# Moving half of a transpose from key tile 1 to key tile 3 in two groups of a two-layer attention kernel

## What is computed

```
xn = layer_norm(x, norm_w, norm_b)
q, k, v = xn @ q_w + q_b, xn @ k_w + k_b, xn @ v_w + v_b      # 16 heads
att = softmax(q k^T + mask)                                   # no scale
y = att v
h = layer_norm(y, sb_norm_w, sb_norm_b) * (1 + scale) + shift # from the condition
x = x + silu(h) @ out_w + out_b
```

## Time and profile before

| | |
|---|---|
| median of three runs | 494.33 us |
| the profiled execution, its own time | 494.05 us |
| its span, first to last instruction | 492.2 us |
| granted TensorE clock | 1.000 |
| PE busy | 481.6 us (98%) |
| DVE busy | 387.1 us (79%) |
| ACT busy | 342.9 us (70%) |
| POOL busy | 314.1 us (64%) |

### The profile page before, as it was taken

The page is one execution under the profiler, slowest core; times in us unless marked ns, Lnnn a source line. Parts: engine busy times, 40 slices in busy tenths (PEclk is TensorE's granted clock), DMA queues, the critical chain, the costliest instruction groups (busy, mean ns, idle before and its releaser), DMA issues.

```text
span 492.2 us, 9721 instructions
## 1 busy us (share of the span) xinstructions
PE 481.6 (98%) x3205; PEld 176.6 (36%) x3205; DVE 387.1 (79%) x990; ACT 342.9 (70%) x676; POOL 314.1 (64%) x447
## 2 busy tenths in 40 slices
PE   8999899999999999999999999999999999999996
PEld 3553322323333234323343234333333323332234
DVE  3767896998887688957887588966899999999224
ACT  1662557898767685967768676776787778777853
POOL 6469976788798987898747881749971055005501
PEclk9999999999999999999999999999999999999999
DMA  7775156344413455234512451114311121111011
GB/s 254 198 200 188 50 149 246 111 124 147 128 49 113 142 149 148 69 87 121 138 39 67 134 159 43 46 46 128 89 45 44 45 88 45 44 45 45 2 43 43
DMA packets 41577, 49.79 MB, mean 101 GB/s; under 512 B 12388, under 2 KB 34036, under 8 KB 41272
## 3 DMA queue, kind: packets, MB, share of 16 engines
q1 hardware_dynamic: 33336, 31.84, 22.6%
q0 software_dynamic: 7904, 16.03, 10.7%
q10 hardware_dynamic: 288, 1.31, 0.8%
HBM read 27.62 MB, written 19.01 MB: 95 GB/s over the span
## 4 chain that ended last, share of the span: by engine, by line
PE 80%; DVE 13%; issue 3%; POOL 2%; ACT 1%; DVEq 0%; POOLq 0%; ACTq 0%
PE bank L602 20%; PE bank L648 12%; PE bank L585 12%; PE bank L576 11%; PE bank L564 9%; DVE masked L958 8%; PE bank L659 6%; PE bank L676 5%; DVE row_max L961 2%; PE bank L633 2%; PE bank L617 1%; PE bank L610 1%; ACT probs L787 1%; PE bank L734 1%; POOL shift L1335 1%
## 5 line engine op out<-in xcount | busy, mean ns | idle before, releaser
L787 ACT ACTIVATE probs<-bank 128x512 f32<-128x512 f32 x512 | 270.8, 600 | 71.6 <-PE bank L576 70.9
L961 DVE TENSOR_REDUCE row_max<-bank 128x1 f32<-128x512 f32 x256 | 160.4, 682 | 38.2 <-PE bank L585 37.9
L585 PE MATMUL bank<-k_s,q_s 64*128 64x512 f16 x512 | 180.9, 382 | 2.2 <-DVE row_max L961 1.2
L958 DVE CUSTOM_DVE_ANT_0 masked<-bank,mask_bias 128x512 bf16<-128x512 f32 x256 | 162.6, 686 | 18.9 <-PE bank L585 18.1
L564 PE MATMUL bank<-q_s,k_s 64*128 64x512 f16 x512 | 151.4, 380 | 0.3
L576 PE MATMUL bank<-shift,kx 64*128 64x512 f16 x512 | 148.7, 376 | 0.0
L602 PE MATMUL bank<-probs,v_aug 128*17 128x512 f32 x1024 | 135.5, 598 | 0.7 <-ACT probs L787 0.7
L585 PEld LDWEIGHTS bank<-k_s,q_s 64*128 64x128 f16 x512 | 46.2, 93 | 158.0 <-DVE row_max L961 66.3
L1238 POOL TENSOR_SCALAR scaled<-row_max 128x16 f32<-128x16 f32 x30 | 7.7, 255 | 87.8 <-DVE row_max L958 49.6
L648 PE MATMUL bank<-xT,wqkv 128*128 128x512 f32 x128 | 61.7, 612 | 0.9 <-DVE xT L1095 0.6
L576 PEld LDWEIGHTS bank<-shift,kx 64*128 64x128 f16 x512 | 46.9, 95 | 32.7
(11 more groups left out here) (122 smaller groups left out, 481.2 us busy)
## 6 DMA issues: line engine op xcount, KB each, us to landing
q_s<-q_parts SPq DMA_DIRECT2D x32, 256.0 KB, 3.6
k_s<-k_parts SPq DMA_DIRECT2D x32, 256.0 KB, 4.3
k_parts<-parts POOLq DMA_DIRECT2D x62, 128.0 KB, 3.2
q_parts<-parts POOLq DMA_DIRECT2D x60, 128.0 KB, 3.0
X<-in_x SPq DMA_DIRECT2D x4, 512.0 KB, 7.4
O<-oT SPq DMA_DIRECT2D x64, 32.0 KB, 2.0
roped<-inverses SPq DMA_DIRECT2D x16, 128.0 KB
y<-X SPq DMA_DIRECT2D x7, 256.0 KB, 2.2
```

Source lines behind the costliest of these rows:

```text
L585: nc.tensor.matmul(bank, m.q_s[slot][rows, i, queries], m.k_s[slot][rows, i, :], start=True, stop=True).then_inc(q.d_made, 1)
L787: act.activation(m.probs[k][:, h, :], bank, ACT.Exp, scale=1.0 if s >= B * NG else float(DH) ** -0.5)\
L958: dve.tensor_tensor_reduce(m.masked[D["max", n, k, h] % ND][:, :], bank, m.mask_bias[:, b, :], 1.0, LOWEST, ALU.add, ALU.max, to)\
L961: dve.tensor_reduce(to, bank, AX.X, ALU.max).then_inc(q.d_done, 1)
```

## The change

In groups 22 and 26 the first half of the turn stays in key tile 0. The second half goes from key tile 1 to key tile 3 of the same group. With it go its DVE operation, its tanh on ACT and its places in DVE's bank ring. The order on POOL is not edited.

```diff
-PIECES[22] = (*one(turn("f1", 0)), (), ())
+PIECES[22] = (turn("f1", 0)[:1], (), (), turn("f1", 0)[1:])
 PIECES[23] = ((), (), y(1, 0)[:1], ())
 PIECES[24] = ((), (), (), y(1, 0)[1:])
-PIECES[26] = (*one(turn("f1", 1)), (), ())
+PIECES[26] = (turn("f1", 1)[:1], (), (), turn("f1", 1)[1:])
```

## The result

Over 20 runs of each, the changed kernel takes 495.51 us (median), the kernel before 494.40: 1.11 us more, ratio 1.0025 with a 95% interval of 1.0017 to 1.0032. The forecast was 495.0, in a range of 493.8 to 495.7. A second comparison, 11 runs of the changed kernel against 27, gave 495.25 against 494.40, ratio 1.0015 (1.0006 to 1.0024). So the change costs something near the 0.2% line: the first ratio lies just over it, where I had 16%, the second under it, and both intervals hold it. In the first comparison 8 of the 20 runs of the changed kernel took over 496 us, against 2 of 20 of the kernel before; without them the medians are 495.20 and 494.40, 0.80 us apart.

A forecast was written before the change was run, and what follows sets the result against it. PE, 98% busy, was taken to bound the kernel. Per group -0.09 - 0.32 + 0.61 + 0.15 = +0.35, so +0.70 us on the profiled 494.05 gives 494.75; with 0.28 to the median, 495.0, range 493.8 to 495.7.

The forecast's parts named there:

- Key tile 1 held by ACT through L610: Group 22: the turn of the shift rows waits for ACT's late probability, so losing 0.60 us of transposes gains only 0.09.
- Key tile 2: Groups 22 and 26: without the second tanh and halving ahead, it falls from 3.42 to about 3.10 us, gaining 0.32.
- Key tile 3: Groups 22 and 26: taking in the half turn, it grows from 2.49 to 3.10 us, losing 0.61.
- Key tile 0 of group 23: Behind the turned key tile, the last score's load waits for ACT's backlog to about 2.02; 0.15 us lost (0 to 0.20).
- POOL: Negated maxima of group 24, needed in key tile 1 of group 23: slack shrinks from 1.9 to 0.3 us but holds.
- A reading that does not carry: Sign in key tile 1: a row score waits for DVE, read as DVE being behind by its second halving.
- The sum: Per group -0.09 - 0.32 + 0.61 + 0.15 = +0.35 us; group 26 the same, so +0.70.
- The gain: Rival: waits in groups 22 and 26 go, nothing replaces them; 0.38 us gained per group, 493.6 us; 12%.
- The draw: Rival: key tile 1 gives back 0.18, group 23's wait is hidden; -0.3 to +0.3 us, 494.3; 12%.
- the further waits: Rival: waits beyond the bounds, such as key tile 3's halving pushing row maxima against the three-bank ring; above +1.0 us; 5%.
- The late POOL: Rival: negated maxima of groups 24 and 28 miss L610 and PE stands; 0.5 us lost per group, 496.0 us; 9%.

The follow-up runs named there:

- the later tanhs: Kernel before, each tanh one step later on ACT: in groups 22 and 26, 493.73 against 494.17 us (repeat 494.18 against 494.40); with group 30 too, 494.87 against 494.47.
- the first-tanh run: Changed kernel, ACT doing the tanh of the first half only behind two probabilities of the next key tile: 494.30 us against 494.47 for the kernel before, ratio 0.9996.
- both tanhs late: Changed kernel with the tanhs of both halves in groups 22 and 26 one step later on ACT: 500.30 us against 494.47 for the kernel before, ratio 1.0106.
- three groups held back: Kernel before with the tanhs of groups 22, 26 and 30 one step later on ACT: 494.87 against 494.47 us; repeated, 494.63 against 494.40.
- group 22 alone: Kernel before with the second half moved in group 22 only, group 26 as before: 494.56 us against 494.17, ratio 1.0010.
- the half in key tile 2: Changed kernel, but the second half in key tile 2 instead of key tile 3 of groups 22 and 26: 494.83 us against 494.17 for the kernel before, ratio 1.0014.
- the changed kernel again: Changed kernel, unaltered, measured a second time against the kernel before: 495.25 us against 494.40, ratio 1.0015.

## Why the prediction was right, and where its sizes were off

*Key tile 1 held by ACT through L610*: right, down to the values starting 0.10 behind L610. It gave 0.06 us for 0.60 of transposes, 0.09 forecast. Two runs show it from both sides: key tile 1 stays at 3.12 when the half goes elsewhere, and falls to 2.56 when ACT is relieved.

*Key tile 2*: 0.33 gained, 0.32 forecast. That ACT and not DVE made most of that wait is shown by the later tanhs (3.42 to 3.15).

*Key tile 3*: 0.61 lost, 0.61 forecast.

*Key tile 0 of group 23*: 0.10 lost, 0.15 forecast, and here the size is partly luck. The wait that I named is there: the load of the last score starts 2.04 behind the end of key tile 3, 2.02 forecast. But it is not what most of the loss hangs on. With the first tanh alone held back the key tile stays at 2.58, and with both held back, where that wait is gone, it is still 2.56. Some 0.08 us come with the second half whatever ACT does, most likely from DVE, which I had taken only as something that could hide ACT's wait.

*POOL*: this is the term that was mis-sized. I put its slack at 0.3 us and its cost at nothing; the slack was some 0.03, and the cost was 0.08 us in a group. Three things ate it: 0.15 for the way from POOL to PE, for which I took nothing; 0.08 by which the maxima end later behind key tile 3 than I had (4.88 us, not 4.80), since I left out the step from the multiplication to the maxima (374.26 to 374.35); and 0.05 by which L610 comes sooner, the key tile before being shorter than forecast. The y product's key tile gave 0.03 back, which I did not foresee.

*A reading that does not carry.* I took the 0.20 us by which a row score waits for DVE in key tile 1 as a sign that DVE is behind there. A key tile without a piece has the same wait:

```profile
371.93 0.09 PEld L585 LDWEIGHTS bank<-k_s,q_s 64*128 64x128 f16 x1 [0.20 <-DVE row_max L958]
```

That DVE holds key tile 1 before the change rests on its busy time there and on the 3.17 us that stay when the tanhs come later.

*The sum*: +0.38 a group, +0.35 forecast; +0.76 us, +0.70 forecast. That it comes so near is in part luck: POOL's 0.08 was missing, and 0.05 too much in key tile 0 of group 23 and the 0.03 of the y product's key tile set it off. The measured median difference was 1.11 in the first comparison and 0.85 in the second. In the first profiled execution 0.31 us of the difference (2.79 against 2.48) arise in key tile 1 of group 7, long before the change, where L610 starts 0.15 behind the end of POOL's maxima (148.71 and 148.86), the way from POOL to PE again: POOL is half a microsecond later there, as the row of the changed kernel shows (147.36 in the kernel before).

```profile
147.88 0.27 POOL L1238 TENSOR_SCALAR scaled<-row_max 128x16 f32<-128x16 f32 x1
```

Over twelve profiles this key tile took 2.48 to 2.79 us in kernels that are all alike up to there, so it varies by itself. Another part of the spread may be the landing of the last output, below; without the runs over 496 us the first difference is 0.80. Whether some of the 0.1 to 0.35 us over 0.76 belongs to the change, and whether the changed kernel has more of the long runs by itself, is open: 0.76 us is a ratio of 1.0015, the very value of the second comparison and just under the interval of the first (from 1.0017).

*The rivals.* The gain is refuted by key tile 1, and the first-tanh run shows what it lacked. The draw wanted 0.18 from key tile 1 and nothing lost in group 23; it was 0.06 and 0.18. A push of the moved halving against DVE's ring, which I had put among the further waits, is what most of the loss in key tile 0 of group 23 looks like, but with 0.08 us and not 0.5. The late POOL happened by 0.08 us in a group and not by the 0.5 of that rival; it sets in when POOL is 0.03 us later and not 0.3, and costs 2.3 us in key tile 1 when it is driven there.

## What to carry to other kernels

An extra step that is taken out of a crowded tile returns its own time only if it was also what the next wait hung on. Here ACT's standing for the first half, in the tile before, set the end, so moving the second half away freed nothing while its 0.6 us had to be paid in full elsewhere. Ask of the tile that loses work which release comes last in it, and of the tile that gains it what stands behind the moved step in every in-order queue, with the measured delay of each signal. Here, to the start of PE's weight load, it was 0.04 to 0.07 us from the end of a probability on ACT and 0.12 us from POOL's last operation, and 0.15 us from that to the matmul.

## What the hardware showed beside that

**A fall of the clock after a second standing.** With both tanhs late PE stands 2.13 us in group 23 and the granted clock stays at 1.00; it stands 2.12 us again in group 27, and the next stretch of that kernel has a granted clock of 0.74, a mixture of the two levels (1.2 and 2.4 GHz). The last two rows are the beginning of that stretch, at the lower level:

```profile
423.09:427.89 4.80, 2.68 (x23) 0.84 (x22) 3.94 (x14) 4.10 (x9) 3.44 (x5) 0.99 0.30 104
427.89:434.28 6.39, 6.39 (x34) 2.72 (x33) 2.45 (x7) 1.46 (x4) 0.00 (x0) 0.74 0.01 1
427.89:429.50 1.61, 1.61 (x9) 0.15 (x8) 0.00 (x0) 0.27 (x1) 0.00 (x0) 0.50 0.00 0
429.50:431.00 1.50, 1.50 (x10) 0.29 (x6) 0.63 (x2) 0.19 (x1) 0.00 (x0) 0.50 0.03 5
```

The key tile takes 6.39 us where it takes 4.85 at full clock: 1.5 us on top of the wait itself. Three of the four executions of this kernel have a mean granted clock of 0.997 and spans of 498.4 to 499.0 us; the fourth has 1.000 and 497.0. So the same standing does not always bring the fall; what decides it is not shown here.

**An instruction fetch in the last transfer.** The profiled execution with three groups held back ends 4.05 us after its last DVE operation has ended (488.95 and 493.0); the kernel before ends 2.2 us after. Its DMA view from 489 to 490 us (queues with packets, MB and share; below them the issue and its landing):

```profile
q1 hardware_dynamic: 165, 0.15, 45.8%
q8 instruction: 1, 0.02, 7.3%
y<-X SPq DMA_DIRECT2D x1, 128.0 KB, 3.6
```

One instruction packet holds one of the 16 DMA engines for about 1.2 us (7.3% of 16 engines' microsecond), and the last output lands after 3.6 us instead of 1.8. Of the twelve profiles, five have such a packet of q8 between 489 and 492 us, amid the last outputs, and in all five the last output lands after 3.2 to 3.7 us and the one before it after 2.0; the seven without it there have 1.7 or 1.8 for both. Three of these five profiled executions (group 22 alone, the half in key tile 2, the changed kernel again) took 1.5 to 1.8 us more than the median of their kernel. That the one causes the other is argued from this agreement; what sets the time of the fetch was not found. The kernel that ends its work at 489 us met it in both profiles, and of its 23 executions only one has a span (491.1 us) near the 491.2 that I had expected without it; so a gain of 1 us made earlier can be lost at the end.
